# Four fused vision layers: the first pass with its first layer run once per half block, the three taps put on ScalarE and VectorE, and fixed slots over three images

## The reference, cut to what matters

```python
mu, var = mean(x, -1), var(x, -1)                         # over 96 channels
x_norm  = (x - mu) / sqrt(var + 1e-5) * gamma + beta
grey    = x_norm.mean(-1)                                 # one value per pixel
scores  = from mean |horizontal difference| and mean |vertical difference| of grey
is_v    = argmax(softmax(relu(scores @ w1 + b1) @ w2 + b2)) == 1      # one flag per image
seq     = (swapaxes(x_norm, 1, 2) if is_v else x_norm).reshape(32, 3136, 96)
t       = seq @ fc1_w + fc1_b                             # 96 -> 192
t       = dw_w[c, 0] * t[n-1] + dw_w[c, 1] * t[n] + dw_w[c, 2] * t[n+1] + dw_b   # per channel c
out     = x + gelu(t) @ fc2_w + fc2_b                     # 192 -> 96
```

## Time and profile before

| | |
|---|---|
| median of three runs | 11909.03 us |
| the profiled execution, its own time | 11907.59 us |
| its span, first to last instruction | 11905.8 us |
| PE, ACT, DVE, POOL busy over the span | 94%, 66%, 62%, 37% |
| mean granted clock of PE | 0.974 of 2.4 GHz |
| first pass: first matmul for a mean to last residual | 76.84 to 2147.96 us |

### The profile page before, as it was taken

One profiled execution on the slowest core, in us unless ns is written; L12 is line 12 of the kernel. 1 busy time (PEld: TensorE's weight loads), 2 busy tenths in 40 slices (PEclk: granted clock), 3 DMA queues, 4 the chain that ended last, 5 costly groups with the idle time before them and its releaser, 6 DMA issues. The chain is left out here.

```text
span 11905.8 us, 393166 instructions
## 1 busy us (share of the span) xinstructions
PE 11196.1 (94%) x157972; PEld 8194.0 (69%) x157972; DVE 7361.0 (62%) x12636; ACT 7836.3 (66%) x13524; POOL 4375.4 (37%) x5892
## 2 busy tenths in 40 slices
PE   6999999899999999998989999998999999999999
PEld 3444444577777777777767676766877778777777
DVE  4444444577777777775456666666666666666665
ACT  4555555477777777775346666765777777777776
POOL 0000000377777777774000000001555555555554
PEclk9999999899999999999989999998999999999999
DMA  1111111122222222223643333332010001010000
GB/s 57 36 40 35 40 40 35 36 52 51 51 51 51 51 51 51 51 51 105 215 122 77 76 78 75 78 76 53 24 24 24 24 24 24 24 25 24 24 24 22
DMA packets 1105618, 617.58 MB, mean 52 GB/s; under 512 B 864651, under 2 KB 1076566, under 8 KB 1099704
## 3 DMA queue, kind: packets, MB, share of 16 engines
q1 hardware_dynamic: 1091496, 553.66, 19.2%
q10 hardware_dynamic: 12288, 38.54, 1.0%
HBM read 308.38 MB, written 282.75 MB: 50 GB/s over the span
## 5 line engine op out<-in xcount | busy, mean ns | idle before, releaser
L1485 POOL TENSOR_TENSOR L_HdL<-L_Hd,L_HdH 128x392 fp32r<-128x392 f32 x1536 | 1572.1, 1024 | 283.9 <-POOL L_HdH L1483 283.2
L1469 POOL TENSOR_TENSOR L_SQ<-L_X 96x392 f32<-96x392 f32 x512 | 429.4, 839 | 2316.0 <-DMA L_X<-after_L 2306.4
L985 PEld LDWEIGHTS banks<-L_ident,L_PR 113*113 113x113 f32 x9216 | 1149.4, 181 | 187.9 <-issue 126.8
L985 PE MATMUL banks<-L_ident,L_PR 113*113 113x113 f32 x9216 | 1204.4, 267 | 1.2 <-DVE L_X L1391 0.7
L1220 ACT COPY L_PT<-banks 113x452 f32<-113x452 f32 x1792 | 886.1, 538 | 414.4 <-PE banks L985 414.1
L1236 ACT ACTIVATE L_PR<-L_SX 113x588 f32<-113x588 f32 x1536 | 1087.5, 708 | 51.5 <-DVE L_SX L1363 10.5
L395 PE MATMUL banks<-scan_XS,scan_W1T 97*96 (+1 forms) x2688 | 1113.2, 553 | 0.0
L1533 POOL COPY L_XN<-L_XR 96x392 f32<-96x392 f32 x256 | 147.6, 577 | 2508.2 <-DMA L_XR<-L_norm 2371.3
L1056 PE MATMUL banks<-L_VB,L_PT 113*49 113x34 f32 x36864 | 1063.9, 213 | 1.4 <-ACT L_PT L1220 1.0
L1483 POOL CAST L_HdH<-L_Hd 128x392 fp32r<-128x392 f32 x1536 | 788.6, 513 | 742.8 <-issue 684.1
L1263 ACT ACT_TABLE_LOAD x512 | 656.9, 1283 | 606.2 <-PE banks L992 606.2
(11 more groups left out here) (233 smaller groups left out, 25901.0 us busy)
## 6 DMA issues: line engine op xcount, KB each, us to landing
L_X<-after_L SPq DMA_DIRECT2D x768, 147.0 KB
after_L<-L_X SPq DMA_DIRECT2D x512, 147.0 KB
conv_T<-L_norm_by_phase SPq DMA_DIRECT2D x96, 512.0 KB, 3.3
L_norm_by_phase<-L_XP SPq DMA_DIRECT2D x512, 84.0 KB, 2.1
scan_XT<-in_x SPq DMA_DIRECT2D x33, 1176.0 KB, 7.0
L_norm<-L_XA SPq DMA_DIRECT2D x256, 147.0 KB, 1.9
L_conv<-conv_D ACTq DMA_DIRECT2D x96, 392.0 KB, 3.0
L_XR<-L_norm SPq DMA_DIRECT2D x256, 147.0 KB, 2.4
```

The costliest lines, as they stand in the source:

```text
L985: mm = pe.transpose(bank(TURN[a])[0:SPAN, (k % 4) * SPAN:(k % 4 + 1) * SPAN], PR[:, st.v if lag else st.u, 2 * k:2 * k + 2, :].rearrange(" ...
L1485: pool.tensor_tensor(HdL[:, u, j].bitcast(F32R), Hd[:, u, j], HdH[:, u, j], ALU.subtract).then_inc(s[f"hd_parts_{j}"], 1)
```

## The change: what it does

The change is confined to `scan_pass` and to the host's layout of the taps.

1. `conv_half` becomes `units`: one matmul per half block, with plain `W1`, over 450 columns (448 and one on each side), into one of two banks. ACT multiplies the middle 448 columns by tap 1 into `U` (`middle`), DVE adds tap 0 times the columns to the left and then tap 2 times those to the right, in place (`side_taps`). ACT's gelu reads `U` instead of the bank.
2. The squares, `normed` and the blend move to POOL. The blend is three instructions per block instead of two.
3. An image passes through three steps instead of two: norm in step i, flag and blend in step i + 1, the two layers in step i + 2. `XM` has four buffers, `XN` two, `Hd` three.
4. ACT takes the logarithms of groups 0 and 1 together, and those of 2 and 3 together, in slots 4 and 10, the exponentials in slots 5 and 11; no gelu is issued in these four slots, they are caught up in slots 6 and 12.
5. The loop is gone: all 35 steps are written out. fc2 and residual of a block follow its first unit by 6 slots.

```diff
-    MEAN_BEFORE, MEAN_BEHIND = {0: 0, 1: 1}, {2: 2, 3: 3}
-    VAR_BEHIND = {1: 0, 2: 1, 4: 2, 5: 3}
-    TURN_SLOTS, DIFFS, SUMS, SCORE, SEL1, SEL2, FLAG = (7, 8), 7, 8, 9, 10, 11, 12
+    MEAN_AT, VAR_AT = {0: 0, 1: 1, 5: 2, 6: 3}, {2: 0, 3: 1, 8: 2, 9: 3}
+    LOGS_AT, EXPS_AT, GELU_AT = {4: (0, 1), 10: (2, 3)}, {5: (0, 1), 11: (2, 3)}, (6, 12)
+    TURN_AT = {11: (0, 1), 12: (2, 3), 13: (4, 5, 6)}
+    DIFFS, SCORE, SEL1, SEL2, FLAG = 2, 3, 4, 5, 7
...
-            + [(taps[0:C + 1, t, :], w["dw_taps"][t:t + 1, :].broadcast_to([C + 1, 2 * C])) for t in range(3)],
+            (taps[:], w["dw_taps"])],
...
-                for t in range(3):
-                    dve.tensor_tensor(W1T[0:C + 1, t, :], W1[0:C + 1, :], taps[0:C + 1, t, :], ALU.mult)
...
-            with eng.Fori(0, B - 2) as k:
-                step(eng.snap(k + 1), True, True, True)
+            for i in range(B + 3):
+                for k in range(SLOTS):
+                    unit = (i - 2) * SLOTS + k
+                    if unit < UNITS + 2 * NB:
+                        step(i, k, i < B, 1 <= i <= B, i + 1 < B, unit)
...
-                    for t in range(3):
-                        mm = pe.matmul(PS[0:C, 4 + k % 3, 0:TB], W1T[0:C + 1, t, h * C:(h + 1) * C],
-                                       xs[:, m * TB + t:m * TB + t + TB], start=(t == 0), stop=(t == 2))
+                    pe.wait_ge(s["xs"], c * NB + min(m + 2, NB))
+                    if unit >= 2:
+                        pe.wait_ge(s["tapped"], unit - 1)
+                    pe.matmul(PS[0:C, Z_BANKS[unit % 2], 0:TB + 2], W1[0:C + 1, h * C:(h + 1) * C],
+                              XS[:, c % 2, m * TB:m * TB + TB + 2], start=True, stop=True).then_inc(s["units"], 1)
...
+                def middle(unit):
+                    act.wait_ge(s["units"], unit + 1)
+                    if unit >= NU:
+                        act.wait_ge(s["gelu"], unit - NU + 1)
+                    act.mul(U[:, unit % NU], PS[0:C, Z_BANKS[unit % 2], 1:TB + 1], taps[:, 1, unit % 2:unit % 2 + 1]).then_inc(s["middle"], 1)
...
+                def side_taps(unit):
+                    h, z, u = unit % 2, PS[0:C, Z_BANKS[unit % 2]], U[:, unit % NU]
+                    dve.wait_ge(s["middle"], unit + 1)
+                    dve.scalar_tensor_tensor(u, z[:, 0:TB], taps[:, 0, h:h + 1], u, ALU.mult, ALU.add).then_inc(s["left"], 1)
+                    dve.wait_ge(s["left"], unit + 1)
+                    dve.scalar_tensor_tensor(u, z[:, 2:TB + 2], taps[:, 2, h:h + 1], u, ALU.mult, ALU.add).then_inc(s["tapped"], 1)
...
-                                dve.scalar_tensor_tensor(target, XNT[:, m * RB:(m + 1) * RB, :], fb[:, 0:1], target, ALU.mult, ALU.add).then_inc(s["xs"], 1)
+                    pool.tensor_scalar(tv.rearrange("c (a q) -> c a q", q=H), XNT[:, m * RB:(m + 1) * RB, :], fb[:, 0:1], None, ALU.mult).then_inc(s["blend"], 1)
+                    pool.tensor_scalar(target, XN[0:C, p % 2, m * TB:(m + 1) * TB], fb[:, 1:2], None, ALU.mult).then_inc(s["blend"], 1)
+                    pool.wait_ge(s["blend"], 2 * (n + 1))
+                    pool.tensor_tensor(target, target, tv, ALU.add).then_inc(s["xs"], 1)
...
+                SQUARE_AT, NORMED_AT = {1: 0, 2: 1, 6: 2, 7: 3}, {6: (0, 1), 13: (2, 3)}
+                BLEND_AT = {8: (0,), 9: (1,), 10: (2,), 11: (3,), 12: (4, 5), 13: (6,)}
```

More of the change, by code:

```diff
@@ new lines, in step @@
+                def step(i, k, norm, sel, turn, unit):
+                    if 0 <= unit < UNITS:
+                        units(unit)
+                    if norm and k in MEAN_AT:
+                        mean(i, MEAN_AT[k])
+                    if norm and k in VAR_AT:
+                        variance(i, VAR_AT[k])
+                    if turn:
+                        for m in TURN_AT.get(k, ()):
+                            turn_block(i + 1, m)
+                    if sel:
+                        if k == SCORE:
+                            hold(pe, s["sums"], i, passed)
+                            pe.matmul(PS[0:4, SEL_BANK, 0:1], GA[:], gone[:], start=True, stop=True).then_inc(s["score"], 1)
+                        if k == SEL1:
+                            hold(pe, s["scores"], i, passed)
+                            pe.matmul(PS[0:16, SEL_BANK, 0:1], sw1[:], sc[:], start=True, stop=True).then_inc(s["sel1"], 1)
+                        if k == SEL2:
+                            hold(pe, s["hidden"], i, passed)
+                            pe.matmul(PS[0:1, SEL_BANK, 0:4], hid[:], sw2[:], start=True, stop=True).then_inc(s["sel2"], 1)
+                        if k == FLAG:
+                            hold(pe, s["flag"], i, passed)
+                            pe.matmul(PS[0:C, SEL_BANK, 0:2], one1[:], fl[:], start=True, stop=True).then_inc(s["flagb"], 1)
+                    if due(unit) is not None:
+                        fc2_block(due(unit))
@@ L521, in _ @@
+                over_slots(step)
             @block.vector
@@ L631, in _ @@
+                    if sel and k == FLAG:
+                        dve.wait_ge(s["flagb"], i)
+                        if i >= 2:
+                            dve.wait_ge(s["xs"], (i - 1) * NB)
+                        dve.tensor_copy(fb[:], PS[0:C, SEL_BANK, 0:2]).then_inc(s["factors"], 1)
+                    if due(unit) is not None:
+                        residual(due(unit))
                 for m in range(NB):
                     copy_turned(0, m)
-                over_images(dve, step)
+                over_slots(step)
```

399 lines of the change are left out of this document (173 added, 226 removed).

## The result

The kernel after took 11831.92 us (median of 4 runs, 11827.24 to 11835.09), the kernel before 11910.39 us on the same chip: a ratio of 0.9932, 95% interval 0.9914 to 0.9949. It is 78 us faster; 509 were forecast. The interval leaves out 1, so the direction was right, but the size and the range were wrong.

The account below looks back on a forecast made before the run. PE was taken to bound the first pass at 64.6 us an image; 28 steps at 48.3 plus the other steps end it at 1639 instead of 2148, gaining 509 for 11400 us; 80% range 11270 to 11525.

Parts of the forecast that it names:

- the stretch of POOL from the factors to the next square: POOL's blends, normed and next square: from 27.0 to 8.8 us into the next image, making PE 2.6 us late.
- term for a block's blend: POOL's three blend instructions per block: 1.18 + 0.77 + 1.06 + 0.19 for the wait, 3.2 us.
- Rival 2: POOL bounds the pass: 4.05 us a blend, square 8.7 us late, 54.4 us an image, 11583 us; chance 15%.
- the ring: Chain of waits from one image's factors round to the next's; the forecast priced this period at 48.3 us.
- Rival 4: PE falls to half clock in the first pass: 77 us an image, 12280 us, slower than before; chance 3%.
- wrong if the clock in the pass is under 0.9: Sign set beforehand for PE's granted clock in the first pass: under 0.9 would show the forecast wrong.
- Unrolling taken at 0: Instruction fetching for the written-out first pass: 0 us taken, up to 3.5 us an image kept inside the range.
- The forecast of 48.3: Period of a middle image in the first pass: 45.7 us of order plus 2.6 us of lateness.
- nothing else changes, so the whole sum is made there: Claim that the first pass alone changes, so the whole gain of 509 us falls there.
- The floor of 2.5: Lower bound for POOL's blend per block: 2.5 us if transposed reads cost nothing and pair operations go at 0.839.
- The order without POOL's lateness: Slot-by-slot schedule of one image in the first pass without POOL: 45.7 us.
- The stride term: POOL's transposed blend multiply: 1.18 us against 0.77 straight, from DVE's ratio of 1.54.

Follow-up runs that it names:

- e8: Kernel after, with POOL's two blend multiplies given a second operation that adds a column of zeros: 11557.04 us.
- e2: Kernel after, with POOL's normed of groups 0 and 1 moved behind the square of group 3: 11774.65 us.
- e5: Kernel after with nothing on POOL: squares moved to ACT and two slots earlier started, normed and blend to DVE: 11662.11 us.
- e11: Kernel after with squares on ACT, two-operation blend multiplies, and POOL's normed of group 0 waiting for the flag: 11436.23 us.
- e4: Kernel after with idle PE matmuls, 16 before the variance of group 0 and 12 before the flag matmul: 11763.93 us.
- e12: e11 plus idle PE matmuls, 6 before an image's first mean and 8 before the flag matmul: 11302.71 us.
- e13: Kernel before, with its loop over images 1 to 30 written out and nothing else changed: 11733.21 us.
- e3: Kernel after with the blend back on DVE in two instructions per block, squares and normed still on POOL: 11783.0 us.
- e6: Kernel after with only the squares moved from POOL to ACT, those of groups 0 and 1 one slot earlier: 11461.16 us.
- e9: Kernel after with the edits of e2 and e4 together, idle matmuls 16 and 8: 11752.48 us.
- e14: e12 with the blend's multiplies on POOL back in the one-operation form: 11449.97 us.

## Why the prediction was wrong

The pass came out 481 us too long (2120.0 for 1639) and what lies behind it 47 us too short; the sum is the miss of 434 us on the profiled execution. Of the 481, 28 x (63.2 - 48.3) = 417 are the middle images, the rest the first and last steps.

1. **The step that failed** is the stretch of POOL from the factors to the next square: "from the factors at 27.0, six blends 19.2, normed of groups 2 and 3 3.2, one blend 3.2: 52.6", and the square "to 8.8", so that PE is "2.6 us late". Its term for a block's blend was too small: it took 1.86 + 1.40 + 1.13 and the handing-on, 4.4 to 4.5 us and not 3.2, so the stretch was 34.3 us and not 25.6. That is 8.7 of the 15.8 us by which an image of 64.1 us is too long. With the one term mended (e8) the stretch is 24.7 us and the middle images take 54.6, still 6.3 too many. Rival 2 had this mechanism ("POOL bounds", 4.05 a block, 54.4 us an image), with 15%; its price was exceeded.
2. **A cost that stood in no term** is in the rest of the ring. From the start of PE's variance to POOL's next blend the forecast has 20.8 us (8.8 to 27.0 + 2.6), and the trace 28.1 (1048.17 to 1076.3). L567 makes 5.3 of these 7.3 us: it took 5.55 us where 0.2 was counted. It took 1.50 with another order (e2) and 0.22 with POOL idle (e5, e11). Not every short step stood. Two of the kernel after (shortest, median and longest ns):

```profile
L561 DVE TENSOR_TENSOR scan_GA<-scan_GA x29: 143/1531/1532, 226.6 to 1995.2; 56x1 f32<-56x1 f32 x29
```
```profile
L566 DVE TENSOR_REDUCE scan_st<-scan_st x28: 145/146/147, 241.6 to 1948.6; 1x1 f32<-1x4 f32 x28
```

L561 adds two columns in SBUF and stood until POOL's square ended; L566 reads one and ran in 0.15 us while POOL's square was on. With L555 (1.02 us for 0.20) and L559 (0.94 for 0.16), which also read two tensors in SBUF, another 3 us an image were spent so. The trace of before could not show it in this pass, since POOL did nothing there. The Trainium skill's GPSIMD Engine Reference (section 8, Key points) says that GpSimd shares its SBUF interfaces with VectorE, and names VectorE instructions in a two-port mode or with two SBUF inputs as those that contend. L555, L559, L561 and L566 agree with it, and so do the taps, which read one operand from PSUM and kept 0.68 us; whether L567, which reads four numbers and a column, is one of the two kinds no run here shows. I had read the page for its stride rule and left that sentence out; it gives no size, and the trace has the sizes above.
3. **The clock.** Rival 4 was priced as all or nothing (66 us an image at least) and so got 3%. It came in part: 0.50 in three stretches an image, behind idle of 4 to 7.5 us. The forecast's test, "wrong if the clock in the pass is under 0.9", was met with 0.81. Its price is 1.6 us an image while POOL rules (e4) and 3.8 once it doesn't (e12).
4. **Unrolling taken at 0.** The fetching shows no cost: the queue for instructions carried 32 packets in 60 to 2070 us, one an image, where the forecast allowed for 7. But the 0 left out a gain: two table loads that the loop brings, one of them readable in the trace of before at 1025.98. The forecast of 48.3 counted four loads and was not touched by it, but the credit was: written out alone, the kernel before gains 182 us, so all else in the change together loses 99 us. What loses them is POOL: the same change with nothing on POOL (e5, 11662.11 us) is 71 us faster than the unrolled kernel alone.
5. **"nothing else changes, so the whole sum is made there"** missed 47 us. In e13 the same passes gain 30 us though only the loop above them was written out. That it is the program's place or its layout is argued, not shown.
6. **Small slips in the sum.** Rival 2's 4.05 does not follow from its row: a blend whose one-input operations go at the cast's rate comes to 3.8. The floor of 2.5 leaves out the 0.19 for the wait. 8.8 less 6.05 is 2.75 and not 2.6.
7. **What held.** DVE's taps (0.68 us), POOL's add (1.05) and normed (2.07), four loads an image, the load's price without a drain, and the first mean (68.4 for 71). POOL's square was cheaper than its 1.9 (1.68). The grey DMA was not free: DVE waited for it 1.6 us an image (31.1 us, 20 times, in 200 to 1500 us). The order without POOL's lateness, 45.7 us, was close: with POOL out of the way and the clock up, the middle images take 46.7 (e12), though with the squares on ACT and 14 idle matmuls. The stride term held too: transposed 1.18 against straight 0.72, a ratio of 1.64, in e8 (1.33 in the one-operation form); the Trainium skill's half more (same page, section 7) is near it.

How much of the 6.3 us that e8 leaves is DVE's standing and how much the low clock stays open: no run took one of them out of that kernel alone.

## What to carry to other kernels

Three edits with one answer each (unroll, split the taps, move to POOL) must be priced apart: here unrolling alone gave 182 us, the split with its new order another 71 (e5), and the move to POOL took 170 back. When work goes to an engine whose order is written out, price the last thing in its queue that the next round waits for, not its busy share: moving the squares away was worth 371 us from an engine that was 67% busy in the pass. And when no engine is saturated, two chains can end at nearly the same point, so removing one shows little (17 us) until the other is gone (147 us for the same form).

## What the runs showed of the hardware

- POOL's tensor_scalar with one operation took 1.40 us for 96 x 448 float32, with a second that adds zeros 0.72 us; with a transposed read 1.87 and 1.18 us. A square of one tensor of 896 columns took 1.68 us, a product of two 2.07 us.
- A DVE instruction on 1 x 4 numbers in SBUF stood up to 5.55 us beside POOL's square and normed, in e3 too, where POOL had little else; a reduction over 4 numbers took 0.15 us beside the same square, and the taps, which read PSUM, did not lengthen (0.68 us). Why it was held once over three POOL instructions (after) and once slipped in between two (e6, 0.32 us) stays open.
- PE's granted clock was at 0.50 behind 3.9 us of idle in e11 (PE busy 84% of 200 to 1500 us); with six idle matmuls in that gap it was back at full speed before the image's first mean had ended (e12).
- The same program of four passes took 9757.8 us behind the looped pass (before) and 9684 to 9728 us behind the 16 unrolled ones. The four with idle matmuls are the lowest of these (9684 to 9701; e4, e9, e12, e14). Why stays open.
